# A post-norm decoder layer with 16 experts: the order of two early loads, and which engine adds epsilon in two layer norms

## What is computed

```python
x = layernorm(x + attention(x))          # one head, 1024 keys, softmax(q k / 16) v, then out_w
x = layernorm(x + cross_attention(x))    # 16 heads over 64 keys of ctx, causal and padding masks
x = layernorm(x + moe(x))                # softmax router, top 4 of 16 experts, gelu FFN 256-512-256
# layernorm(x) = (x - mean) / sqrt(var + 1e-5)
```

## Time and profile before

| | |
|---|---|
| median of 3 runs | 586.83 us (585.78 to 587.88) |
| the profiled execution: its own time | 587.42 us |
| the profiled execution: span of the trace | 585.6 us |
| PE, DVE, ACT, POOL busy in the span | 93%, 68%, 55%, 46% |
| PE busy from 80 to 150 us (self-attention) | 69.99 of 70.00 us |
| PE busy from 185 to 207 us (cross-attention) | 22.00 of 22.00 us |

### The profile page before, as it was taken

How to read it: one execution, slowest core, us unless ns; L and a number is a source line. 1 busy time by engine, 2 the same in 40 slices (tenths; PEclk the granted TensorE clock), 3 DMA queues, 4 the chain that set the end, 5 groups by cost and what they waited for, 6 DMA issues and landing times.

```text
span 585.6 us, 14223 instructions
## 1 busy us (share of the span) xinstructions
PE 546.6 (93%) x4048; PEld 505.4 (86%) x4048; DVE 399.3 (68%) x898; ACT 321.6 (55%) x658; POOL 269.9 (46%) x255
## 2 busy tenths in 40 slices
PE   5999999999998989989789999999999999999774
PEld 4988998888987978878678899999999999999752
DVE  2636656656567747778334598878789779878754
ACT  2424333333345535554355678777778767977505
POOL 6650000000013646555636545576576575557713
PEclk9999999999998979989979999999999999999988
DMA  8699999980000312323848989999999999999494
GB/s 271 227 385 385 385 385 386 386 290 0 1 1 22 106 73 82 116 81 118 271 141 252 293 229 271 269 258 247 263 252 252 263 259 243 263 254 237 55 279 157
DMA packets 91558, 127.49 MB, mean 218 GB/s; under 512 B 6708, under 2 KB 62708, under 8 KB 91528
## 3 DMA queue, kind: packets, MB, share of 16 engines
q1 hardware_dynamic: 76328, 107.23, 55.1%
q0 software_dynamic: 14304, 19.67, 16.5%
q10 hardware_dynamic: 896, 0.23, 0.2%
HBM read 62.59 MB, written 64.52 MB: 217 GB/s over the span
## 4 chain that ended last, share of the span: by engine, by line
PE 63%; issue 12%; DMA 9%; DVE 5%; ACT 4%; another core or an unknown queue 2%; POOL 2%; ACTq 1%; POOLq 0%; DVEq 0%; SPq 0%
PE ps L395 12%; PE ps L397 11%; PE ps L396 11%; DMA expert_sum<-yb,home_row 8%; PE ps L970 3%; PE ps L897 3%; PE ps L1092 2%; PE ps L1078 2%; PE ps L933 2%; PE ps L962 2%; PE ps L954 2%; PE ps L1014 1%; PE ps L1219 1%; PE ps L1018 1%
## 5 line engine op out<-in xcount | busy, mean ns | idle before, releaser
L704 POOL DMA_INDIRECT expert_sum<-yb,home_row x76 | 150.3, 1977 | 88.0 <-DVE home_row L1931 49.6
L395 PE MATMUL ps<-gT_h,w_h 128*128 128x256 f32 x288 | 83.6, 290 | 1.3 <-issue 1.3
L395 PE MATMUL ps<-w_h,h_h 128*128 128x256 f32 x288 | 81.6, 283 | 1.9 <-DVE h_l L1917 1.6
L397 PE MATMUL ps<-w_h,h_l 128*128 128x256 f32 x288 | 81.4, 283 | 0.0
L396 PE MATMUL ps<-w_l,h_h 128*128 128x256 f32 x288 | 81.3, 282 | 0.0
L397 PE MATMUL ps<-gT_h,w_l 128*128 128x256 f32 x288 | 80.6, 280 | 0.0
L396 PE MATMUL ps<-gT_l,w_h 128*128 128x256 f32 x288 | 80.5, 280 | 0.0
L650 POOL DMA_INDIRECT expert_rows<-x_all,idx x64 | 63.2, 987 | 34.4 <-issue 29.9
L634 POOL TENSOR_TENSOR rstd<-ve,mhalf 128x1 f32<-128x1 f32 x16 | 8.8, 553 | 116.3 <-DVE ve L1650 116.3
L1917 DVE TENSOR_TENSOR h_l<-hf,h_h 128x1024 fp32r<-128x1024 f32 x35 | 42.9, 1225 | 23.8 <-ACT h_h L1489 17.0
L1482 ACT ACTIVATE hf<-ps,b1s 128x256 f32<-128x256 f32 x140 | 55.1, 489 | 5.2 <-PE ps L397 5.1
(11 more groups left out here) (300 smaller groups left out, 1414.0 us busy)
## 6 DMA issues: line engine op xcount, KB each, us to landing
expert_rows<-zeros SPq DMA_DIRECT2D x32, 1152.0 KB, 14.3
w1f<-in_L_ffn_w SPq DMA_DIRECT2D x40, 512.0 KB
w2f<-in_L_ffn_w SPq DMA_DIRECT2D x40, 512.0 KB
xg<-expert_rows SPq DMA_DIRECT2D x40, 288.0 KB
expert_sum<-zeros SPq DMA_DIRECT2D x10, 256.0 KB, 9.9
x_all<-in_x SPq DMA_DIRECT2D x8, 256.0 KB, 7.2
expert_sum<-x_all SPq DMA_DIRECT2D x8, 256.0 KB
total<-expert_sum SPq DMA_DIRECT2D x4, 512.0 KB, 5.8
```

The source lines that it names most:

```text
L395: pe.matmul(o, ah, bh, start=first, stop=False)
L397: return pe.matmul(o, al, bh, start=False, stop=last)
L704: pool.indirect_dma_start(out=sums[p], out_offset=bass.IndirectOffsetOnAxis(ap=home_row1[:, t, c:c + 1] if early else home_row[:, p, c:c + ...
```

## The change

Two edits. On SP, the load of the first two tiles of x is issued ahead of the load of the query and key weights, not behind it. In both attentions, the addition of epsilon to the variance moves from DVE to POOL, directly ahead of the root; POOL now waits for the statistics (`bna`, `cbna`) and then for its own addition (`var`, `cvar`).

```diff
@@ SP
             sp.dma_start(n_out[:], out_w...).then_inc(ld_out, 16)
-            sp.dma_start(n_qkv[:, 0:2 * KD], qkv_w[0:2 * D]...).then_inc(ld_qk, 16)
...
             load_x(0)
+            sp.dma_start(n_qkv[:, 0:2 * KD], qkv_w[0:2 * D]...).then_inc(ld_qk, 16)
             sp.dma_start(n_qkv[:, 2 * KD:3 * KD], qkv_w[2 * D:3 * D]...).then_inc(ld_v, 16)
@@ POOL
             def root(t, p, k):
+                pool.wait_ge(bna, done(t))
+                pool.sem_inc(passed, 1)
+                pool.tensor_scalar(ve[:, p:p + 1], mv[:, p, 1:2], EPS, None, ALU.add).then_inc(var, 1)
                 pool.wait_ge(var, done(t))
                 pool.tensor_tensor(rstd[:, p:p + 1], ve[:, p:p + 1], mhalf[:], ALU.pow).then_inc(rst, 1)
...
             def root2(t, p, k):
+                pool.wait_ge(cbna, done(t))
+                pool.tensor_scalar(ve[:, p:p + 1], mv[:, p, 1:2], EPS, None, ALU.add).then_inc(cvar, 1)
                 pool.wait_ge(cvar, done(t))
@@ DVE
                 dve.bn_aggr(mv[:, p], bn[:, p]).then_inc(bna, 1)
-                dve.wait_ge(bna, done(t))
-                dve.tensor_scalar(ve[:, p:p + 1], mv[:, p, 1:2], EPS, None, ALU.add).then_inc(var, 1)
...
-            def var2(t, p, k):
-                dve.wait_ge(cbna, done(t))
-                dve.tensor_scalar(ve[:, p:p + 1], mv[:, p, 1:2], EPS, None, ALU.add).then_inc(cvar, 1)
...
-                     (3, aggr2), (4, slots), (3, var2), (4, indices), (4, share_sum), (4, all_shares)]
+                     (3, aggr2), (4, slots), (4, indices), (4, share_sum), (4, all_shares)]
```

More of the change, by code:

```diff
@@ L419, in _ @@
             sp.dma_start(n_out[:], out_w.rearrange("(k p) c -> p k c", p=P)).then_inc(ld_out, 16)
-            sp.dma_start(n_qkv[:, 0:2 * KD], qkv_w[0:2 * D].rearrange("(k p) c -> p k c", p=P)).then_inc(ld_qk, 16)
             def load_x(t):
@@ L425, in _ @@
             load_x(0)
+            sp.dma_start(n_qkv[:, 0:2 * KD], qkv_w[0:2 * D].rearrange("(k p) c -> p k c", p=P)).then_inc(ld_qk, 16)
             sp.dma_start(n_qkv[:, 2 * KD:3 * KD], qkv_w[2 * D:3 * D].rearrange("(k p) c -> p k c", p=P)).then_inc(ld_v, 16)
@@ L1841, in _ @@
                       (4, rows_of), (4, chosen_rows), (4, share_sum), (4, slots), (4, all_shares), (4, indices),
-                      (3, stats2), (3, aggr2), (3, var2), (4, early_homes)]
+                      (3, stats2), (3, aggr2), (4, early_homes)]
             pipeline(dve, NT, order + [(4, table_early)], ramp=ramp, ramp_steps=2 * B + 1, ending=ending, unrolled=UNROLLED, written=ROUNDED_OUT)
```

## The result

The changed kernel takes 579.92 us (median of 20 executions, 576.1 to 586.72), the kernel before 583.65 beside it on the same chip (579.56 to 588.4). The ratio is 0.9937, 95% interval 0.9917 to 0.9957: 3.7 us (2.5 to 4.8) are gained. Single executions of one kernel differ by 9 to 11 us, so one trace shows where something happens and hardly how much it is worth. Ratios leave out the executions that ran over 1.5% above the fastest of their kernel, and the profiled execution of after, 585.77 us (span 584.0), is such a one.

The account below looks back on a forecast made before the run. PE was taken to set the pace in both attentions. Load edit -1.1 us, epsilon 0 in self-attention and +0.1 in cross-attention: from the median, 586.83 - 1.0 = 585.8 us, range 582.3 to 588.6.

Parts of the forecast that it names:

- Edit 1, the start: Front of the program: x turned from 5.6 us, L815 begins at 7.1 instead of 8.26, 1.15 us earlier.
- Rival 4: Front loads: transfers interleave, x and weights both land at 7.1 us, so the first edit does nothing: 586.9 us; chance 0.08.
- Edit 1, how much is kept: Front of the program: of the earlier start 0.6 to 1.8 us are kept, 1.1 taken as the plain shift.
- The bound from below: First eight products (L815): if the clock rises at the same moment, near 10.45 us, only 0.6 us are kept.
- Edit 2 in self-attention: Sixteen tiles: gain 0; POOL's addition takes 0.2 us, the root starts 0 to 0.1 later, under 0.8 to spare.
- Edit 2 in cross-attention: Sixteen tiles: +0.1 us; DVE gains nothing, POOL's round grows to 6.15, under PE's 6.8.
- PE sets the pace: Both attentions: PE busy 69.99 of 70.00 us (80 to 150) and 22.00 of 22.00 (185 to 207); DVE waits.
- The two waits of the earlier trace: Cross-attention: PE idles 2.74 us ahead of 210.09 and 4.87 ahead of 294.61; no mechanism given, they widen the range.
- The sign that I had named for being wrong: Cross-attention: PE's idle time between 200 and 300 us differs by over 1.5 us, in either direction.
- Rival 1: Cross-attention: scatter bursts shift against PE's steps, late releases shrink, 3 to 5 us gained, 581.0 to 583; chance 0.23.
- Rival 2: Cross-attention: late releases move against us, one more wait of 2.7 plus up to 3.4 us, 588.5 to 591.9; chance 0.14.
- Rival 3: Cross-attention: POOL's additions hold DVE instructions with two SBUF inputs, up to 3.3 us, 589; chance 0.03.

Follow-up runs that it names:

- warm: The changed kernel plus twelve early PE products of the identity with itself, meant from 1.5 us on: 581.0 us, 0.9935 of the kernel before.
- eps_self_only: The kernel before with the addition of epsilon moved to POOL in self-attention only: 584.42 us, ratio 0.9996.
- pool_gap1: The kernel before with one idle POOL addition between root and scatters of each cross-attention tile: 578.43 us, ratio 0.9966.
- pool_gap4: The kernel before with four idle POOL additions between root and scatters of each cross-attention tile: 575.98 us, ratio 0.9917.
- eps_both: The kernel before with epsilon added on POOL, while DVE still does its own additions into a spare tile: 577.34 us, ratio 0.9948.
- before_2: The kernel before, unchanged, run under another name as if it were a change: 582.32 us, ratio 1.0037.
- eps_2: Second run of the kernel before with only the epsilon addition moved to POOL, in both attentions: 582.57 us, ratio 0.9945.
- eps_none: The kernel before with no addition of epsilon on any engine, the root taken of the bare variance: 583.97 us, ratio 1.0055.
- mid_gap: The kernel before with five idle POOL additions between the second and third scatter of each cross-attention tile: 571.98 us, ratio 0.9869.
- full_2: The changed kernel, run a second time against the kernel before: 581.4 us, ratio 0.994.
- best_each1: The kernel before with the load edit, twelve early PE products, and one idle POOL addition behind each of the first three scatters: 565.54 us, 0.9742.
- split: The changed kernel with POOL taking the next cross-attention tile's addition and root between a tile's second and third scatter: 619.63 us, 1.0685 of the kernel before.

## Why the prediction was wrong

The gain came out at 3.7 us and not 1.0. The 579.92 us lie below the range of 582.3 to 588.6; set against the median that I started from, the ratio gives 586.83 * 0.9937 = 583.1, just inside it.

- **Edit 1, the start.** Right: x is turned at 5.55 us (said 5.6) and L820 starts at 6.99 (said 7.1). Rival 4 is out.
- **Edit 1, how much is kept.** Mis-sized. I took the plain shift, 1.1 us; seventeen traces give 0.6, give or take 0.5, at L834 and again at 170 us. The bound from below was built on the clock rising at the same moment (0.6), and that was nearly the case that came. The early rise came only when PE was given work from 1.56 us on: in `warm` L822 ends 2.0 us earlier than L815 before (9.04 and 11.08; I had said 2.2), but at L395 1.3 us of it are left. By the ratios the load edit alone is worth 1.6 us, give or take 1.6. Whether what is above 0.6 is chance or a shift against the bursts, as with epsilon, stays open.
- **Edit 2 in self-attention.** Right: 0.24 us on POOL (said 0.2), PE busy 69.99 of 70.00, eps_self_only 0.9996.
- **Edit 2 in cross-attention, +0.1 us.** This is the step that failed, in its sign. Each of its parts holds. `ve` filled a gap; after, L1787 starts as far behind L1783 as L1788 behind L1784 before:

```profile
281.00 0.18 DVE L1783 MAX8 at<-posm 128x8 f32<-128x16 f32 x1
281.21 0.17 DVE L1787 TENSOR_SCALAR idx<-at 128x4 uint32<-128x4 f32 x1
```

  POOL's round grew by 0.17 us, from 5.92 to 6.09 (first scatters at 200.26 and 206.35), where I said 6.15. But the sum priced POOL's time as load, under PE's round and so free. What counts is when a burst stands against PE's releases, and there a later start gains: 0.8 to 3.2 us in the four kernels with the addition on POOL and the loads as before (0.9976, 0.9986, 0.9945, 0.9948; the first two not told apart from 1), 2.0 with idle work in its place (0.9966), 4.8 with more of it (0.9917).
- **What bounds the kernel.** "PE sets the pace" in both attentions was wrong for the second. I read it from 185 to 207 us, where PE has 22.00 of 22.00; from 185 to 285 it has 92.60 of 100, at 0.95 of the clock, and broken bursts with the two edits at the front win 15 us back in all. The two waits of the earlier trace rows were the visible end of it. The sign that I had named for being wrong is there too. From 200 to 300 us, before and then after, PE stands still for 1.66 us less:

```profile
200.00:300.00 100.00, 87.73 (x616) 77.21 (x616) 64.51 (x247) 47.20 (x133) 54.16 (x60) 0.92 0.36 126
```

```profile
200.00:300.00 100.00, 89.39 (x616) 77.93 (x613) 63.60 (x230) 46.49 (x132) 57.99 (x72) 0.93 0.36 126
```

- **Rival 1, the late releases move in our favour**, was the case that came, at the slow edge of its 581 to 583 us (583.1 by the ratio). I gave it 0.23 and wrote against it that nothing in the edit makes the bursts shorter. They needn't be shorter. Rival 2, the same mechanism with the other sign, had the same row behind it, and nothing in the trace of before told the two apart. That the sign came out as a gain was not derived.
- **Rival 3**, that POOL's additions hold DVE, is not seen. The longest L1756 is the first again:

```profile
L1756 DVE TENSOR_TENSOR mk<-rest,lg x16: 174/176/609, 180.3 to 301.9; 128x16 fp32r<-128x16 f32 x16
```

  It ends at 180.9 with POOL's long select, as the one before did. Two others take 245 and 227 ns, at 220.00 and 243.23, where POOL starts a scatter and not an addition. The Trainium skill (GPSIMD Engine Reference, Key points) says that the two engines contend when VectorE has two SBUF inputs. The 609 ns agree; the sixteen additions of 128 numbers left no trace.
- **Sums.** Three were slightly off. The forecast's own fast end, 1.8 us gained and 0.1 lost, is 585.1 and not 584.9; rival 1, 3 to 5 us under 585.8, is 580.8 to 582.8; and what the range left out is about 0.25 of chance, not under 0.2. None of them moves the forecast.

What stays open. That late releases come with POOL's bursts, and that they go when the bursts are broken or halved, is shown. That the epsilon edit gains through the later start is shown by its likes (pool_gap1, pool_gap4, eps_both), not by a count in single traces: "remote" waits of DVE are 10.5 us in 6 before, 8.1 in 5 in before_2, and 8.2 in 6 after, 11.1 in 9 in eps_2, so one execution of each doesn't tell them apart. Many together lean its way: with DVE's and ACT's from 175 to 305 us added, the mean is 30.4 us (23.7 to 37.2) in the six traces with POOL's work in the cross-attention as before (eps_none among them), and 25.5 (18.5 to 29.9) in the seven with its addition there. How large its gain is stays loose, 2.3 us give or take 1.5. Whether the release itself is held up, or TensorE's products really end later than the profile's modelled ends, these traces can't tell; either way the waiting engine starts late. Why a burst does this was not tried, nor was a kernel in which the rows are sent without POOL.

## What to carry to other kernels

When an engine waits for something that by the trace ended microseconds ago, don't put it down as noise: look what runs on every other engine in that gap, and try to break that up. Here three short idle instructions in each burst of indirect DMAs, with two small edits at the front, were worth four times the change under study; idle additions in the burst alone (mid_gap) were worth twice. Judge whether a stage is bound by an engine over the whole stage, waits and granted clock included, and not by a stretch in which it happens to be full. And where the sign of an edit hangs on how two engines' phases fall, price it as a case of its own with both signs, not as its instructions' time.

## What the runs showed of the hardware

- Around GpSimd's back-to-back indirect DMAs (0.96 us each, 0.30 apart), what VectorE and ScalarE await from TensorE reaches them up to 3.0 us behind the product's end in the rows above, 5.8 near 290 us. In self-attention, without scatters, PE is busy 69.99 of 70.00 us. With one addition of 0.23 us behind each of the first three scatters DVE has no such wait from 185 to 285 us, and ACT one.
- TensorE's granted clock in the first stage did not follow the first real products when they started 1.0 us earlier (3.78 us for the eight in four of five traces, 2.98 to 3.62 without the edit), but with products from 1.56 us on it had risen by 6 us (four transposes in 0.60 us and not 1.08).
- The cost of the lower level is spread: over all executions the median of the mean granted clock is 0.979 in before_2, 0.984 in full_2, 0.990 in mid_gap, 0.992 in best_each1 and 0.9475 in split, in the order of their times; pool_gap4 with 0.9885 is faster than pool_gap1 with 0.9895, so the clock is not all of it. In the trace of before it falls at 208.3 us, after PE had stood still from 207.35, and the eight products of L954 take 1.91 us at 210.68 where they took 1.02 at 200.78. How much of the 15 us is the waits and how much the lower clock was not separated.
